# Products between keys inside blocks of four tokens: their diagonal gathered by transfers through DRAM instead of by masks and selecting products

## The reference, cut to what matters

```python
q, k, v = silu(conv(x @ Wq.T)), silu(conv(x @ Wk.T)) * DK ** (-0.5), silu(conv(x @ Wv.T))
a, beta = sigmoid(x @ Wa.T + ba), sigmoid(x @ Wb.T + bb)
def step(S, xs):                      # one token; S is [b, h, v, k]
    q_t, k_t, v_t, a_t, b_t = xs
    Sk = einsum('bhvk,bhk->bhv', S, k_t)
    S = a_t[..., None] * S - (b_t[..., None] * (Sk - v_t))[..., None] * k_t[:, :, None, :]
    return S, einsum('bhvk,bhk->bhv', S, q_t)
```

## Time and profile before

| | |
|---|---|
| median of 3 runs | 2856.45 us |
| profiled execution, its own time | 2844.69 us |
| its span, first to last instruction | 2843.0 us |
| TensorE clock granted, mean over the span | 0.890 |
| recurrence, 925.1 to 2440 us of the span | 1514.90 us |
| one chunk, by slots, 1311.90 to 1407.73 us | 95.83 us |
| the next chunk | 98.72 us |

### The profile page before, as it was taken

One profiled execution on the slowest core, in us unless ns is written; L12 is line 12 of the kernel. 1 busy time (PEld: TensorE's weight loads), 2 busy tenths in 40 slices (PEclk: granted clock), 3 DMA queues, 4 the chain that ended last, 5 costly groups with the idle time before them and its releaser, 6 DMA issues.

```text
span 2843.0 us, 67669 instructions
## 1 busy us (share of the span) xinstructions
PE 2215.3 (78%) x24976; PEld 1672.4 (59%) x24976; DVE 1919.1 (68%) x4412; ACT 1323.3 (47%) x2752; POOL 558.7 (20%) x546
## 2 busy tenths in 40 slices
PE   5999888888882776877787777768777875489998
PEld 3455666666662666776676666667666764234443
DVE  5223877787771888878888878787888888423334
ACT  2001666666662444644454455445444643144434
POOL 0000232333334122212222212222222222100000
PEclk9999999999996889978888898789888887699999
DMA  5001354445457234334433443343334333401210
GB/s 223 8 9 43 148 213 190 194 195 213 192 193 276 91 124 139 121 93 142 138 120 101 138 146 108 115 133 121 123 124 136 120 100 129 155 0 74 74 59 22
DMA packets 139483, 358.77 MB, mean 126 GB/s; under 512 B 11312, under 2 KB 92968, under 8 KB 126424
## 3 DMA queue, kind: packets, MB, share of 16 engines
q1 hardware_dynamic: 139176, 354.92, 35.1%
q0 software_dynamic: 48, 0.16, 0.0%
HBM read 226.97 MB, written 128.07 MB: 125 GB/s over the span
## 4 chain that ended last, share of the span: by engine, by line
PE 48%; issue 20%; DVE 12%; ACT 9%; POOL 6%; DMA 3%; DVEq 0%; SPq 0%; ACTq 0%; POOLq 0%
PE PS L1306 9%; PE PS L1345 4%; PE PS L1416 4%; PE PS L1443 4%; ACT arena L680 3%; PE PS L1169 3%; PE PS L1294 3%; PE PS L1217 3%; POOL arena L487 2%; PE PS L1333 2%; PE PS L1320 2%; DMA arena<-beta_d 2%; PE PS L1265 2%; DVE arena L979 2%; DVE arena L985 2%
## 5 line engine op out<-in xcount | busy, mean ns | idle before, releaser
L1192 PE MATMUL PS<-arena 128*128 x2048 | 491.0, 399 | 97.3 <-DVE arena L886 96.2
L886 DVE SCALAR_TENSOR_TENSOR arena<-PS,SM,arena 128x256 f32<-128x256 f32 x1152 | 468.5, 476 | 123.6 <-ACT arena L596 120.8
L1192 PEld LDWEIGHTS PS<-arena 128*128 128x128 f32 x2048 | 395.8, 195 | 192.5 <-DVE arena L886 112.5
L1306 PE MATMUL PS<-arena 128*128 128x128 f32 x1920 | 301.5, 304 | 92.0 <-ACT arena L685 90.6
L525 POOL TENSOR_TENSOR arena<-arena 128x256 f32<-128x256 f32 x128 | 98.6, 770 | 1180.9 <-DVE arena L985 1180.9
L1306 PEld LDWEIGHTS PS<-arena 128*128 128x128 f32 x1920 | 253.7, 206 | 130.4 <-ACT arena L685 116.8
L680 ACT ACTIVATE arena<-arena 128x128 f32<-128x128 f32 x960 | 302.1, 395 | 0.0
L596 ACT ACTIVATE arena<-PS,SM 128x256 f32<-128x256 f32 x384 | 207.6, 565 | 151.4 <-PE PS L1192 147.8
L660 ACT COPY arena<-PS 128x512 f32<-128x512 f32 x154 | 90.2, 586 | 382.1 <-PE PS L1233 192.4
L929 DVE TENSOR_TENSOR arena<-arena,PS 128x512 f32<-128x512 f32 x192 | 127.4, 684 | 155.1 <-PE PS L1345 154.3
L1320 PE MATMUL PS<-arena 32*128 32x128 f32 x1920 | 161.6, 314 | 28.6 <-DVE arena L935 28.6
(11 more groups left out here) (138 smaller groups left out, 3873.7 us busy)
## 6 DMA issues: line engine op xcount, KB each, us to landing
arena<-g_d SPq DMA_DIRECT2D x128, 512.0 KB, 4.3
vas_d<-arena SPq DMA_DIRECT2D x24, 2048.0 KB, 6.9
arena<-vas_d SPq DMA_DIRECT2D x128, 384.0 KB, 3.3
kq_d<-arena SPq DMA_DIRECT2D x8, 4096.0 KB, 11.4
arena<-kq_d SPq DMA_DIRECT2D x16, 2048.0 KB, 9.9
arena<-beta_d SPq DMA_DIRECT2D x8, 2048.0 KB, 8.4
kb_d<-arena SPq DMA_DIRECT2D x8, 2048.0 KB, 13.9
arena<-kb_d SPq DMA_DIRECT2D x16, 1024.0 KB, 6.3
```

The lines of the kernel that those rows point to most:

```text
L886: nc.vector.scalar_tensor_tensor(acc, raw[:, :, i:i + PT_], CW[:, w, i, hh:hh + 1], acc, ALU.mult, ALU.add).then_inc(job_free if i == TAPS ...
L1192: ins = mm(dst.rearrange("p (b n) -> p b n", b=B), W4[:, w, kt, DH * h:DH * (h + 1)], XNT[:, kt, :, bass.ds(c * PT_ + (HALO - halo), halo ...
L1306: ins = mm(bank(7)[:, 128 * gi:128 * (gi + 1)].rearrange("v (l x) -> v l x", l=NB), STR[:, s % 2, gi, :], KQ[d][:, :, p0:p0 + 2].rearrange ...
```

## The change: what it does

G0 now has room for both halves, and ACT copies the unmasked products there (slots 1 and 3). Four stores write their 128 rows of 512 numbers to DRAM (`r_d`), the row 4q+s at offset 2072q + 520s. Read back with a row pitch of 520, row 4q+s begins 8q numbers further to the left than it was written, so the same 8 columns of each group of 64 are the wanted diagonal. Four transfers from DRAM to DRAM (`gather`) copy them, 256 runs of 32 bytes each, to g_d. A block's numbers are now 32 for each pair, not 16: the load is 1024 KB, and there are two buffers, not four; it is issued when POOL has read the buffer. `PREP_AT` has nothing in slots 2 and 4.

```diff
-PREP_AT = [[("g2", 0), ("g2", 1)], [("g0", 1), ("g4", 1)], [("sel", 2), ("sel", 3)], [("g0", 0), ("g4", 0)], [("sel", 0), ("sel", 1)],
+PREP_AT = [[("g2", 0), ("g2", 1)], [("g0", 1), ("g4", 1)], [], [("g0", 0), ("g4", 0)], [],
            [("gl", 16), ("kt", 0)], [("gl", 8), ("kt", 1)], [("kt", 2), ("kt", 3)]]
-BY_ACT = ("g2", "sel", "kt")
+BY_ACT = ("g2", "g0", "kt")
...
-        GB = take(4 * 16 * NP).rearrange("v (s p x) -> v s p x", s=4, x=16)
+        GB = take(2 * 32 * NP).rearrange("v (b p s e t) -> v b p s e t", b=2, s=4, e=2, t=4)
-        GS = take(2 * 512).rearrange("r (w x) -> r w x", w=2)
-        G0 = take(512)
+        G0 = take(2 * 512).rearrange("r (w x) -> r w x", w=2)
...
             def load_gb(n, m):
-                sp.wait_ge(g_stored[m // 2 % 2], n * 32 + (16 * (m // 4) + 16))
-                sp.dma_start(GB[:, m % 4].rearrange("v p x -> v (p x)"), g_d[at(n), 16 * NP * m:16 * NP * (m + 1)].to_broadcast([128, 16 * NP])).then_inc(gb_in[m % 4], 16)
+                sp.wait_ge(g_stored[m // 4], n * 64 + 64)
+                sp.dma_start(GB[:, m % 2].rearrange("v p s e t -> v (p s e t)"),
+                             g_d[at(n), 32 * NP * m:32 * NP * (m + 1)].to_broadcast([128, 32 * NP])).then_inc(gb_in[m % 2], 16)
+            def store_products(w, item):
                 sp.wait_ge(pa_done, item)
+                for s in range(4):
+                    rows = r_d[w:w + 1, 520 * s:520 * s + 32 * 2072].rearrange("o (r x) -> (o r) x", x=2072)[:, 0:512]
+                    sp.dma_start(rows, G0[s:128:4, w]).then_inc(r_stored, 16)
+            def gather(n, w, count):
+                sp.wait_ge(r_stored, count)
+                for j in range(4):
+                    src = r_d[w:w + 1, 16576 * j:16576 * j + 32 * 520].rearrange("o (r x) -> (o r) x", x=520)[:, 0:512]
+                    dst = g_d[at(n), 32 * NP * 4 * w:32 * NP * 4 * (w + 1)].rearrange("o (a j r x) -> (o j) a r x", a=8, j=4, r=32)
+                    sp.dma_start(dst[j], src.rearrange("r (a z) -> a r z", z=64)[:, :, 0:8]).then_inc(g_stored[w], 16)
...
                 for m in range(NB):
-                    for x in items_of(m, nxt):
-                        if x[0] == "sel":
-                            store_gs(n if x[1] >= 2 else n + 1, x[1], a_item(n, x, nxt))
-                    if m < NB - 2:
-                        load_gb(n, m + 2)
-                    elif nxt:
-                        load_gb(n + 1, m + 2 - NB)
+                    if m == 2:
+                        gather(n, 1, n * 128 + 128)
+                    if m == 4 and nxt:
+                        gather(n + 1, 0, n * 128 + 192)
...
+                    sp.wait_ge(o_step, n * 24 + 3 * m + 1)
+                    if m < NB - 2:
+                        load_gb(n, m + 2)
+                    elif nxt:
+                        load_gb(n + 1, m + 2 - NB)
                     sp.wait_ge(o_ready, n * NB + m + 1)
...
+                    if m == 1:
+                        store_products(1, a_item(n, ("g0", 1), nxt))
+                    elif m == 3 and nxt:
+                        store_products(0, a_item(n, ("g0", 0), nxt))
...
-                    tt(OT, Xc[:, m, :, 0, :], GB[:, m % 4, :, 12:16], ALU.mult).then_inc(o_step, 1)
+                    own = GB[:, m % 2].rearrange("v p s e t -> v p (s e t)")[:, :, 4::9]
+                    tt(OT, Xc[:, m, :, 0, :], own, ALU.mult).then_inc(o_step, 1)
...
-                        a, w = (0, 6, 10)[t], 6 - 2 * t
-                        tt(TMP[:, :, 0:w], GB[:, sl, :, a:a + w], W[:, :, t].unsqueeze(2).to_broadcast([128, NP, w]), ALU.mult).then_inc(wg_mul, 1)
+                        tt(TMP[:, :, 0:6 - 2 * t].rearrange("v p (e t) -> v p e t", e=2), GB[:, m % 2, :, t, :, t + 1:4],
+                           W[:, :, t].unsqueeze(2).unsqueeze(3).to_broadcast([128, NP, 2, 3 - t]), ALU.mult).then_inc(wg_mul, 1)
```

More of the change, by code:

```diff
@@ L76 @@
 READ_AT = [[], [], [0, 1, 2], [3, 4, 5], [6, 7, 8], [9, 10], [11, 12, 13], [14, 15]]
-PREP_AT = [[("g2", 0), ("g2", 1)], [("g0", 1), ("g4", 1)], [("sel", 2), ("sel", 3)], [("g0", 0), ("g4", 0)], [("sel", 0), ("sel", 1)],
+PREP_AT = [[("g2", 0), ("g2", 1)], [("g0", 1), ("g4", 1)], [], [("g0", 0), ("g4", 0)], [],
            [("gl", 16), ("kt", 0)], [("gl", 8), ("kt", 1)], [("kt", 2), ("kt", 3)]]
 KEYS_AT = [None, (4, 1), None, (4, 0), None, (16, 0), (8, 0), None]
-IN_LAST = [("g0", 1), ("g4", 1), ("sel", 2), ("sel", 3)]
-BY_ACT = ("g2", "sel", "kt")
+IN_LAST = [("g0", 1), ("g4", 1)]
+BY_ACT = ("g2", "g0", "kt")
 A_ITEMS = [x for items in PREP_AT for x in items if x[0] in BY_ACT]
@@ L86 @@
 NA, ND, NK = len(A_ITEMS), len(D_ITEMS), len(K_ITEMS)
-A_FIRST, D_FIRST, K_FIRST = 2, 4, 3
+A_FIRST, D_FIRST, K_FIRST = 1, 3, 3
 def slot_pairs(s):
@@ L107, in build @@
     e_d = dram("e_d", (NS, 128, 7 * NP))
-    g_d = dram("g_d", (NS, NB * 16 * NP))
+    g_d = dram("g_d", (NS, NB * 32 * NP))
+    r_d = dram("r_d", (2, 128 * 520 + 2080))
     o_d = dram("o_d", (NS, 128, NB, BP))
@@ L174, in build @@
         TMP = take(6 * NP).rearrange("v (p x) -> v p x", x=6)
-        GS = take(2 * 512).rearrange("r (w x) -> r w x", w=2)
-        G0 = take(512)
-        SEL = take(16 * 32).rearrange("r (s j m) -> r s j m", s=4, j=4)
-        SELM = take(24)
+        G0 = take(2 * 512).rearrange("r (w x) -> r w x", w=2)
         OT = take(BP).rearrange("v (p t) -> v p t", t=BL)
@@ L270, in build @@
         tr_psum, tr_ready, rd_psum, x_read = sem("tr_psum"), sem("tr_ready"), sem("rd_psum"), sem("x_read")
-        sel_step, kc_ready = sem("sel_step"), sem("kc_ready")
+        r_stored, kc_ready = sem("r_stored"), sem("kc_ready")
         pa_full, pa_done, pd_full, pd_done = sem("pa_full"), sem("pa_done"), sem("pd_full"), sem("pd_done")
@@ L398, in _ @@
                 load_vas(0, m)
-            for w in range(2):
-                store_gs(0, w, w + 1)
+            store_products(0, 1)
+            gather(0, 0, 64)
             for m in range(2):
@@ L537, in chunk @@
                         pool.wait_ge(vas_in[0], n * 32 + 16)
-                        pool.wait_ge(gb_in[0], n * 32 + 16)
+                        pool.wait_ge(gb_in[0], n * 64 + 16)
                     outputs(m)
@@ L653, in evac @@
                 src = bank(bk)
-                if what == "sel":
-                    dst = GS[:, which % 2]
+                if what == "g0":
+                    dst = G0[:, which]
                 elif what == "kt":
@@ L663, in _ @@
             key_copy(0, 4, 0)
-            for w in range(2):
-                evac("sel", w, 2 + w, w + 1)
+            evac("g0", 0, 0, 1)
+            act.wait_ge(pd_full, 1)
+            key_copy(0, 16, 0)
             act.wait_ge(pd_full, 2)
-            key_copy(0, 16, 0)
-            act.wait_ge(pd_full, 3)
             key_copy(0, 8, 0)
@@ L716, in next_evac @@
                             what, w = x
[L717 to L720, removed]
+                            if what == "g0":
+                                act.wait_ge(r_stored, n * 128 + 64)
                             evac(what, w, b, a_item(n, x, nxt))
@@ L898, in _ @@
             dve.wait_ge(masks, 3)
[L899 to L910, removed]
+            key_mask(GL[4][:, 0:256], 1, 4, 1)
+            key_mask(GL[16], 0, 16, 2)
+            key_mask(GL[8], 1, 8, 3)
             def chunk(n, i, c, nxt, nxt2):
@@ L973, in weigh @@
                         if t == 0:
-                            dve.wait_ge(gb_in[sl], n * 32 + (16 * (m // 4) + 16))
+                            dve.wait_ge(gb_in[m % 2], n * 64 + (16 * (m // 2) + 16))
                             dve.wait_ge(v_add, k4 + 1)
@@ L1031, in chunk @@
                     for bk, (what, w) in enumerate(items_of(m, nxt)):
[L1032 to L1035, removed]
+                        if what == "g4":
                             key_mask(GL[4][:, 256 * w:256 * (w + 1)], bk, 4, d_item(n, (what, w)))
@@ L1206, in _ @@
                         ins.then_inc(a_full, 1)
[L1208 to L1219, removed]
             def key_transposes(q, c, bk):
@@ L1256, in level_products @@
                                      KQ[c][:, l0:l0 + nl, p0:p0 + size].rearrange("k l p e t -> k l (p e t)"), start=True, stop=True)
-                ins.then_inc(pd_full, 1)
+                ins.then_inc(pa_full if what == "g0" else pd_full, 1)
             def carried(hf):
@@ L1272, in _ @@
             level_products("g4", 0, 0, 1, 1)
[L1273 to L1276, removed]
+            pe.wait_ge(pa_done, 1)
             level_products("gl", 16, 0, 0, 2)
+            pe.wait_ge(pd_done, 1)
             level_products("gl", 8, 0, 1, 3)
             pe.wait_ge(zeros, 5)
-            pe.wait_ge(pa_done, 2)
-            pe.wait_ge(pd_done, 4)
+            pe.wait_ge(pd_done, 3)
             for hf in range(2):
@@ L1352, in prep @@
                         pe.wait_ge(corr_sub, n * N_SUB + (10 if m == 0 else N_SUB if m == NB - 1 else SUB_AT[m]))
-                    if what == "sel":
```

(3 more changed lines are left out.)

3 lines of the change are left out of this document (removed).

## The result

The changed kernel took 2885.04 us (median of 4 runs, 2878.82 to 2890.97), the kernel before 2854.57 beside it: ratio 1.0108, 95% interval 1.0073 to 1.0142. It is slower by 1.1%, where 2791 us was forecast and 2848 was the end of the range. The profiled execution took 2881.43 us, 36.7 more than that of before.

The account below looks back on a forecast made before the run. No engine was full; engines waiting for each other set the time. Terms of 1.7 + 2.4 + 0.2 + 0.6 - 0.5 = 4.4 us a chunk gave 65.5 us, so 2791 us, range 2764 to 2848.

Parts of the forecast that it names:

- rival 1: Slots 2 and 3: PE, with less work, falls to 1.2 GHz; 1.4 of 4.4 us a chunk stay, 2835 us; chance 0.15.
- the argument against it: Slots 2 and 4: removed products are narrow, full ones stay in slot 2, and slot 4's PE pause of 2.85 us goes.
- Slot 2, -1.7: Slot 2: without selecting products PE's reads L1306 start earlier; 1.7 us a chunk saved, ends 1.3 and 2.5.
- Slot 4, -2.4: Slot 4: without products held by DVE's L929, PE's corrections come early; DVE's whole wait, 2.4 us a chunk, is saved.
- Slots 5 and 6, -0.8: Slots 5 and 6: PE leaves slot 4 earlier, so DVE waits less; 0.2 and 0.6 us a chunk saved.
- `weigh`, 0.10 us: DVE reads GB in other steps: 0.10 us more a slot, 0.5 us a chunk on the path (0 to 1.5).
- Transfers at nothing: Stores, gather and 1024 KB loads add nothing to the path; gather taken as 4 us, with 14 us free.
- Rival 2: Slot 4: the gather takes over 14 us, block 4's load lands late and DVE waits; 2910 us at 22 us; chance 0.13.
- The last chunk, 0.5 slower: The last chunk reads no state and DVE sets its slots: 0.5 us slower, once.
- The sum: Whole kernel: 4.4 us a chunk, 66.0 us in 15 chunks, less 0.5: 65.5 us saved, to 2791 us.
- The prediction's own test: Signs of being wrong: DVE waiting for a slot 4 transfer, gather over 14 us, or slots 2 and 3 under 0.8 clock.

Follow-up runs that it names:

- E9: Kernel before with three idle full 128x128x128 products at each place in PE's waits, selecting products kept: 2799.80 us, ratio 0.9807.
- E10: Changed kernel with four idle full 128x128x128 products at each place in PE's waits and five in slot 1: 2755.55 us, ratio 0.9662.
- E2: Changed kernel with 28 unread products a group put back, written to bank 7 so slot 4 need not wait for DVE's L929: 2828.66 us, ratio 0.9919.
- E1: Changed kernel with 28 unread products a group put back at the selecting products' old places, behind the same wait: 2863.8 us, ratio 1.0032.
- E11: Kernel before with four idle full 128x128x128 products at each place in PE's waits and five in slot 1: 2822.07 us, ratio 0.9907.
- E4: Changed kernel with two idle full 128x128x128 products between a piece's transposes and reads, and two behind `corr_transposes`: 2828.98 us, ratio 0.9913.

## Why the prediction was wrong

**The failed step is the weighing of rival 1**, the clock, at 0.15, and the argument against it: "what is removed are narrow products, what stays in slot 2 are full 128 x 128 ones". The first group of selecting products was in 10 of 15 chunks the stretch in which the clock came up. Without them slot 2 stood at 0.56 on average, not 0.79, and slot 3 at 0.85, not 0.96. The rows on record had the sign: in the earlier trace rows the first eight records of L1217 take 0.82 us and those of the second group 0.48. I compared slot 4's 0.89 with the 0.48 and passed over the 0.82, so I took the low level for something that comes of slot 4's pause. That half of the objection failed too: the pause went, and slot 4's clock was 0.88, not 0.90, and slot 5's 0.85, not 1.00. The rival's place and mechanism were right (slot 2's reads at the low level, slot 3 longer), and so was its price for these two slots (3.0 us, measured 3.1); the rest of the loss lies in slots that it kept free. Against the forecast's terms slot 2 paid 2.2 (forecast -1.7, measured +0.5), slot 3 0.9, slot 5 1.1 (-0.2, +0.9), slot 6 0.9 (-0.6, +0.3), and slots 0, 1 and 7 another 1.8, of which the forecast had 0.3 as `weigh`.

**Slot 2, -1.7.** Right only near the clock that the kernel before has there: 10.76 to 10.95 us at 0.80 to 0.82, where before took 12.69 at a mean of 0.79, 1.9 less. At 1.00 it is 0.2 (10.19 in E9, 10.00 in E10). The 3.38 us of DVE's wait that the term rested on were mostly the low clock's own: in those chunks of E9 DVE waits 0.66, and there is little left to gain. In the changed kernel that wait was to fall to about 1.7; it is 3.5 in the mean of 15 chunks, 3.2 before.

**Slot 4, -2.4.** Measured 2.25 in the mean; DVE does not wait before slot 5. The term was about a wait for a bank, which E2 shows by itself.

**Slots 5 and 6, -0.8.** Lost in the changed kernel, with the clock at 0.85 and 0.93. At a clock of 1.00, E10 beside the kernel before, they are -0.13 and -0.42.

**`weigh`, 0.10 us.** 372 ns beside 290, so 0.08; t = 0 and 1 pay nothing (552 and 424 ns, 550 and 424 before):

```profile
L982 DVE TENSOR_TENSOR arena<-arena 128x384 f32<-128x384 f32 x128 | 70.7, 552 | 1.5 <-DMA arena<-g_d 1.5
...
L982 DVE TENSOR_TENSOR arena<-arena 128x256 f32<-128x256 f32 x128 | 54.3, 424 | 3.3
...
L982 DVE TENSOR_TENSOR arena<-arena 128x128 f32<-128x128 f32 x128 | 47.7, 372 | 2.8
```

**Transfers at nothing.** Right: 5.3 us at most for the gather, against 2.7 to 9.1. The 1024 KB load lands after 5.1 us, not 6.3. Rival 2 is out.

**The last chunk, 0.5 slower.** 1.0: from its first `dec` to the end of DVE's last copy L1031, 79.18 us, where before took 78.14. Half of it is slot 2 (9.78, not 9.30); the other slots are 0.06 to 0.09 longer each, which is `weigh`'s 0.08.

**The sum.** With idle products in both, the change is worth 23 to 67 us, best against best 44 (E9 to E10), two thirds of the 65.5. That it comes so near the forecast is partly luck: of the 3.2 us a chunk between the two, slot 4 is 1.9 and slot 6 0.5, but slot 2's 0.8 is for the most part three chunks in which E9's clock stood at 0.81 there, since at equal clock it is 0.2. Between the changed kernel and the one before, without idle products, the clock took more than all of it. The prediction's own test, "slots 2 and 3 at a mean clock under 0.8", was met by slot 2 alone. What stays open: the 0.3% by which E1 is behind the kernel before (slots 0, 6 and 7 in the table), of which only the 0.08 a slot of `weigh` is measured; why slot 0 is longer; and why the clock phases of E11's slot 4 (0.88 in 10 of 15 chunks, where E9 had 3) turned out worse with one product more.

## What to carry to other kernels

When a change takes work away from PE, ask of every stretch at which clock it starts and which instructions run when it comes up; do not count a product as free to remove because it is narrow or hidden. Read the clock slot by slot before and after, not as one mean, and price a stretch at both levels (here eight reads 1.16 or 2.08 us). Then put idle products into PE's waits and find the count by measurement: they were worth more here (4.5% on the changed kernel, 1.9% on the one before) than the work that was saved.

## What was not expected of the hardware

PE at 87% busy (11.96 of 13.81 us in chunk 3) with no wait over 0.7 us between its groups in slot 2's reads stayed at 1.2 GHz through the whole slot in 12 of 15 chunks. In E10 the same slot ran at 1.00 with 16 idle products (32 records) in its waits, where the 112 records of the selecting products had given 0.83 before; E10 also came out of slot 1 at a higher clock (0.83, not 0.60). The Trainium skill ("TensorE: Matmul & The Clock Gate", "A second HAM failure mode: psum-queue depth-cycling") says that short idle times between groups of matmuls, if frequent enough, make the clock swing between its two levels. The runs go the same way, in that work put into such waits of 0.67 us raised slot 2's clock from 0.56 to 0.73 (E4); but in the 12 chunks the clock did not swing within the slot, it stayed low.

A transfer within DRAM of 1024 runs of 32 bytes, issued in four parts over 3.4 us, was through 1.8 us after its last issue or sooner, at 9 ns of a DMA engine for each run.
